# Moving six steps of an attention loop one or two heads later in two engines' instruction streams

## What is computed

```python
def _w8a8_linear(x, w, b):              # rows and weights rounded to 8 bits
    qx, sx = _dyn_quant(x); qw, sw = _quant_weight(w)
    return jnp.einsum('bnc,oc->bno', qx, qw) * (sx * sw[:, 0]) + b

q = _w8a8_linear(layernorm(x), wq, bq)  # 16 heads of 32
k = cond @ wk.T + bk; v = cond @ wv.T + bv
scores = jnp.einsum('bhnd,bhld->bhnl', q, k) * inv_sqrt_d + mask[:, None]
attn = jax.nn.softmax(scores, axis=-1)
o = jnp.einsum('bhnl,bhld->bhnd', attn, v)
x = x + _w8a8_linear(o, wo, bo)
```

## Time and profile before

| what | us |
|---|---|
| median of 3 runs | 725.24 (724.66 to 728.22) |
| the profiled execution, device time | 727.98 |
| its span in the profile | 725.9 |
| attention heads in the span | 338.8 to 496 |
| one batch of the inner ones | 19.50 |
| TensorE busy, whole span | 533.6 (74%) |
| DVE busy, whole span | 365.1 (50%) |
| ACT busy, whole span | 295.0 (41%) |
| POOL busy, whole span | 179.8 (25%) |

### The profile page before, as it was taken

How to read it: one execution, slowest core, us unless ns; L and a number is a source line. 1 busy time by engine, 2 the same in 40 slices (tenths; PEclk the granted TensorE clock), 3 DMA queues, 4 the chain that set the end, 5 groups by cost and what they waited for, 6 DMA issues and landing times. The chain is left out here.

```text
span 725.9 us, 11288 instructions
## 1 busy us (share of the span) xinstructions
PE 533.6 (74%) x3590; PEld 376.3 (52%) x3590; DVE 365.1 (50%) x962; ACT 295.0 (41%) x631; POOL 179.8 (25%) x211
## 2 busy tenths in 40 slices
PE   0060569999999999357999999994083089999991
PEld 0040557677777768233766666663073055555540
DVE  5727747755865766254677777762422022222220
ACT  4056623344344343042788888883010022222220
POOL 1001013232321322003244444423103502222221
PEclk9995569999999999758899999997555589999996
DMA  8959600000000000310122232331401515555534
GB/s 332 423 167 358 190 0 12 11 0 11 11 11 0 11 0 1 138 28 0 50 74 71 78 88 89 106 97 48 171 1 57 159 46 88 89 88 89 89 44 119
DMA packets 23075, 62.59 MB, mean 86 GB/s; under 512 B 3938, under 2 KB 9858, under 8 KB 20986
## 3 DMA queue, kind: packets, MB, share of 16 engines
q1 hardware_dynamic: 18622, 53.47, 22.1%
q0 software_dynamic: 4416, 8.63, 7.7%
HBM read 46.40 MB, written 17.32 MB: 88 GB/s over the span
## 5 line engine op out<-in xcount | busy, mean ns | idle before, releaser
L602 ACT ACTIVATE pE<-sN,nmx 100x361 f32<-100x361 f32 x128 | 77.5, 606 | 5.6 <-DVE nmx L1179 5.6
L1179 DVE CUSTOM_DVE_ANT_0 sN<-ps,maskS 100x361 f32<-100x361 f32 x128 | 62.5, 531 | 27.2 <-issue 13.4
L798 PE MATMUL ps<-ident,pE 100*121 100x100 f32 x384 | 61.8, 285 | 6.5 <-ACT pT L593 6.5
L798 PEld LDWEIGHTS ps<-ident,pE 100*121 100x121 f32 x384 | 49.5, 188 | 28.6 <-issue 18.4
L928 PE MATMUL ps<-VS,hTe 118*128 x120 | 56.7, 609 | 5.5 <-ACT hTe L640 5.5
L503 POOL DMA_INDIRECT sums_out<-yb,backI x20 | 31.1, 1554 | 108.8 <-ACT yb L650 104.8
L593 ACT COPY pT<-ps 121x300 f32<-121x300 f32 x128 | 51.4, 403 | 8.8 <-PE ps L798 8.3
L1294 DVE TENSOR_TENSOR hb<-ps,b1B 128x352 f32<-128x352 f32 x20 | 10.5, 524 | 87.8 <-PE ps L914 87.8
L914 PE MATMUL ps<-CT,xT 128*128 x160 | 52.8, 474 | 2.0 <-DVE xT L1280 2.0
L914 PEld LDWEIGHTS ps<-CT,xT 128*128 128x128 f32 x160 | 31.2, 197 | 24.9 <-issue 12.8
L1061 DVE TENSOR_REDUCE tk<-h 100x1 f32<-100x512 f32 x32 | 20.0, 679 | 40.2 <-ACT h L553 40.1
(11 more groups left out here) (237 smaller groups left out, 1177.6 us busy)
## 6 DMA issues: line engine op xcount, KB each, us to landing
VS<-in_w SPq DMA_DIRECT2D x8, 1024.0 KB, 9.3
CT<-in_ctxT SPq DMA_DIRECT2D x8, 728.0 KB, 16.6
CT<-in_ew SPq DMA_DIRECT2D x8, 704.0 KB
VS<-in_ew SPq DMA_DIRECT2D x8, 672.0 KB
slots_in<-zeros SPq DMA_DIRECT2D x5, 1056.0 KB, 12.4
xin<-slots_in SPq DMA_DIRECT2D x20, 264.0 KB, 3.4
XR<-in_x SPq DMA_DIRECT2D x1, 1600.0 KB
summB<-summary_rows SPq DMA_DIRECT2D x8, 200.0 KB
```

The source lines that it names most:

```text
L602: act.activation(pE[0:S, q, 0:T], sN[0:S, q, 0:T], ACT.Exp, scale=-1.0, bias=nmx[0:S, h_:h_ + 1], accum_out=sums[0:S, j, h_:h_ + 1]).then_ ...
L798: mm = pe.transpose(ps[0:TC, 4 + r, c * S:(c + 1) * S], pE[0:S, h_ % HPC, c * TC:(c + 1) * TC], ident[0:S, 0:S])
L1179: dve.tensor_tensor_reduce(out=sN[0:S, q, 0:T], in0=ps[0:S, q, 0:T], in1=maskS[0:S, j, 0:T], scale=-1.0, scalar=3.4e38, op0=ALU.add, op1=A ...
```

## The change

Three steps of ACT and three of TensorE (four calls of it) are issued at a later head. On ACT: `rows_out` behind head 3 instead of 2, `turned_x` behind head 8 instead of 6, `turned_o` behind head 12 instead of 11. On TensorE: `rows_back` at head 3 instead of 2, `turn_rows(xq2b)` at 6 instead of 5, `queries` at 8 instead of 7, `out_rows` at 12 instead of 11. Inside a head of TensorE the order is: scores of the next group (heads 0, 4, 8, 12), the head's turn, the mix, then these steps. So `queries` comes behind the scores of the last group and the turn of head 8 instead of ahead of them, `out_rows` comes behind the next batch's first scores and the turn of head 12 instead of ahead of them, and `turn_rows(xq2b)` comes behind HOLD and the turn of head 6. `turn_rows(oQb)` stays at head 10. Nothing is added or removed, DVE, POOL and SP are not touched, and `turned_x` for batch 0 stays ahead of the loop.

```diff
@@ -604,11 +604,11 @@
                     at_turn = behind(b, h_ - TURN, first)
                     if at_turn:
                         copy_turned(*at_turn)
-                    if h_ == 6 and not last:
+                    if h_ == 8 and not last:
                         turned_x(b + 1)
-                    if h_ == 2 and not first:
+                    if h_ == 3 and not first:
                         rows_out(b - 1)
-                    if h_ == 11 and not first:
+                    if h_ == 12 and not first:
                         turned_o(b - 1)
 
             def rows_out(b):
@@ -830,23 +830,23 @@
                     turn_head(b, h_)
                     if h_ % HPC == 1 and b * KC + g:
                         mix_group(*divmod(b * KC + g - 1, KC))
-                    if h_ == 2 and b:
+                    if h_ == 3 and b:
                         rows_back(b - 1)
-                    if h_ == 5 and b < B - 1:
+                    if h_ == 6 and b < B - 1:
                         pe.wait_ge(sem("xq2b"), b + 2)
                         pe.wait_ge(sem("o_norm"), after(b))
                         turn_rows(xq2b, "xq2_t", b + 1)
                     if h_ in (5, 9, 13):
                         for i in range(HOLD):
                             pe.matmul(ps[:, 6, KC * S:512], ident[:, :], ident[:, 0:512 - KC * S], start=True, stop=True)
-                    if h_ == 7 and b < B - 1:
+                    if h_ == 8 and b < B - 1:
                         queries(b + 1)
                     if h_ == 10 and b:
                         pe.wait_ge(sem("oQb"), after(b))
                         if b < B - 1:
                             pe.wait_ge(sem("q_taken"), b + 2)
                         turn_rows(oQb, "oq_t", b - 1)
-                    if h_ == 11 and b:
+                    if h_ == 12 and b:
                         out_rows(b - 1)
 
             def hold_clock(products):
```

## The result

The changed kernel is slower: 729.22 us median against 726.96, ratio 1.0031 (95% interval 1.0018 to 1.0044). On the chip of the first experiments its ratio was 1.0053 (1.0033 to 1.0073). The forecast was 1.7 us less, the result is 2.3 us more: within 0.5%, but on the other side.

The account below looks back on a forecast made before the run. Bound: a chain from engine to engine through ACT's three waits, no engine full, 19.50 us a batch. Six inner batches -0.7, last -1.5, first +0.4, together -1.8: from 725.24 to 723.5 us, range 719.5 to 730.

Parts of the forecast that it names:

- The chain: Inner batch, second scores to the next second scores, summed from old-trace distances across engines: 19.4 us instead of 19.5.
- Every new wait that was named: In the inner batch, DVE waits for `rows_back`, queries (0.4) and output product; `q_ready` holds the next first scores (0.6).
- The last batch: Last batch of the stage: ACT's waits at `rows_out` and `turned_o` saved whole, -1.5 us.
- The first: First batch of the stage: rescaling comes later, half hidden by TensorE's order, +0.4 us (0 to 1).
- the distance from `finish1` to head 8: On DVE in an inner batch, taken from the kernel before as 2.99 us.
- `finish5` to head 0: On DVE, into the next batch: 0.85 us without the wait for scores, at most 1.02.
- rival E: TensorE's 1.1 us idle ahead of the last scores lowers its clock: 1.5 a batch, +9, 734 us; chance 0.07.
- Rival D: Output product's delay reaches the next batch's heads in full, 1.0 a batch, 730 us, if rescaling starts after 12; chance 0.12.
- Rivals B: TensorE's own order sets the inner batch's period, without `q_ready` holding it: 18.8 us, total -5.3, 720 us; chance 0.16.
- rival C: ACT's waits simply go, 2.7 us a batch, total -17.7, 707.5 us; TensorE's busy share is no ceiling; chance 0.03.

Follow-up runs that it names:

- the POOL edit: Changed kernel with POOL's sum of rows and output bias (`with_bo`) moved behind the scaling of the queries: 723.13 us, ratio 0.9981 to the kernel before.
- the mark: The changed kernel with no edit, run on the chip of the first experiments: 728.29 us, ratio 1.0053 to the kernel before.
- the last two runs: Changed kernel, `turned_o` and `out_rows` back at head 11, idle products of head 9 moved to 7; the second also without head 13's: 718.63 and 716.20 us.

## Why the prediction was wrong

| distance from the second scores | forecast | changed kernel | with the POOL edit |
|---|---|---|---|
| exponential of head 3 | 1.69 | 1.77 | 1.77 |
| `finish1` | 3.83 | 3.91 | 3.91 |
| DVE's head 8 | 6.82 | 7.34 | 6.92 |
| last scores | 8.84 | 9.38 | 8.96 |
| rescaling | 11.05 | 11.58 | 11.16 |
| next first scores | 14.20 | 14.73 | 14.31 |
| output product | 15.40 | 15.92 | 15.50 |
| `finish5` | 16.50 | 16.99 | 16.57 |
| next head 0 on DVE | 17.35 | 17.72 | 17.30 |
| next second scores | 19.40 | 19.76 | 19.34 |

**The chain was right.** Every new wait that was named is there: for `rows_back` 0.7, for the queries 0.4 (forecast 0.4), `q_ready` ahead of the first scores (0.5; 0.6), `finish5` on the output product. The last batch gained 1.52 (forecast 1.5). The first lost 0.27 between runs whose first batch stayed at the full clock (17.07 with before's order, 17.34 with the new), forecast 0.4.

**The step that failed is the distance from `finish1` to head 8:** 2.99 taken from the kernel before, 3.43 measured. All later rows carry this 0.44 and the 0.08 by which the exponential of head 3 came late; `finish5` to head 0 gave 0.12 back, 0.73 instead of 0.85. The 2.99 holds only where POOL's bias starts 0.94 ahead of the rounding, as it did before; in the changed kernel it starts 0.51 ahead. The prediction had both times, the bias ending at about 6.9 and the rounding, which lies some 2.0 behind `finish1`, at 5.8, and compared the bias only with the reader of its result, wanted at 8.6. It did not ask what runs beside it on the other engine. The POOL edit brings the batch to 19.34 to 19.52, which is the forecast 19.4, and the whole to 0.9981; the forecast was 723.5 / 725.24 = 0.9976. The distances with the POOL edit, the last column, follow the forecast to 0.12. So without this one term the sum of a batch is right. That the whole agrees too needs one thing more: no inner batch of that run was at the lower clock either.

**The second miss is the clock, rival E,** given 0.07. Its mechanism is shown: the gap of 1.2 us where it was forecast at 1.1, the fall behind it, and its going away with products in the gap. In the two profiles of the changed kernel it strikes two of the six inner batches, 1.0 to 1.6 us a time, not 9 in all. Against the 4.1 us between forecast and result, the late bias makes 2.1 and the clock about the rest (2.6 in the profile); how often it falls over many executions no profile here shows, only the 3.1 us that the run with a filled gap is below the mark. The example that the prediction gave for it, batch 0 of the kernel before, is a weak one: there the clock falls at about 344.5, behind shorter idle times of TensorE (0.81, 0.27, 0.35).

**Rival D** named the right culprit, the output product behind the scores, with a rule that did not decide: the rescaling came before 12, at 11.58, and the product still cost about 0.9 a batch: 0.5 of it its own delay (19.34 to 19.52 with the POOL edit against 18.9 with the product ahead of the scores) and 0.4 the late bias that it brings about. The wrong question was whether the three moves together gain; run one at a time, they are two that gain 0.17 and 0.43 and one that takes more than both.

**Rivals B and C** are out: TensorE does wait ahead of the next first scores, and ACT's waits didn't go, they moved. Whether TensorE's busy time is a ceiling, the doubt beside rival C, no run settles: batches of 18.04 were reached, with one set of idle products less, and TensorE was busy for 17.19 of them.

## What to carry to other kernels

Waits that lie in one chain are not a budget: remove one and see where it comes back, step by step, and judge each moved step alone. A duration taken over from the old trace is only good if the same work runs beside it; set the times of DVE's and POOL's instructions side by side in the new order. Work that only holds the clock belongs where its engine waits anyway, and a new gap on TensorE has a price of its own.

## What the runs showed of the hardware

A `tensor_scalar` of DVE, 100 x 512 f32, takes 0.48 to 0.49 us alone and 1.05 when it starts 0.51 behind a POOL addition of 1.28. In the 14 profiles it starts 0.50 to 0.94 behind the addition in 84 batches, takes 0.61 to 1.07 and always ends 0.27 to 0.29 behind POOL's end. DVE's reductions (0.67 to 0.69) and the masked pass (0.52 to 0.54) took no longer beside POOL than elsewhere.

TensorE's clock fell to 0.50 behind single idle times of 1.2 us in a loop that is otherwise 89% busy, in some batches and not in others of the same execution: two of six inner batches in each profile of the changed kernel, three of six in the one with the queries back. Behind an idle time of 1.37 in batch 0 it fell in one of the last two runs and not in the other. In the other eleven profiles TensorE has no idle time over 1.02 in an inner batch, and no fall began in one, though in four of them the clock fell in batch 0. I had thought of it as a risk for the whole loop or none.
